# Second attention: scatter rounds one step earlier, and routing places and weights ahead of one clip

## The reference, cut to what matters

```python
x = x + _L1_xattn_ref(_layernorm(x), ctx_2048, mask, ...)    # 16 heads of 16, scores clipped to +-50
x = x + _L1_ffn_ref(_layernorm(x), gate_w, ...)
# in _L1_ffn_ref: E = 32 experts, K = 4 chosen for each token
logits = x @ gate_w.T + gate_b
topk_logits, topk_idx = jax.lax.top_k(logits, K)
topk_weight = jax.nn.softmax(topk_logits, axis=-1)
order = jnp.argsort(flat_idx)      # rows sorted by expert, then expert products, then summed with the weights
```

## Time and profile before

| what | value |
|---|---|
| median of 3 runs | 1764.74 us (1764.31 to 1765.02) |
| profiled execution, its own time | 1765.31 us |
| its span (first to last instruction) | 1763.6 us |
| second attention with routing, from the first apply to the start of the experts | about 1088 to 1431 us of the span |
| busy over the whole span | PE 86%, DVE 76%, ACT 61%, POOL 60% |

### The profile page before, as it was taken

The page is one execution under the profiler, slowest core; times in us unless marked ns, Lnnn a source line. Parts: engine busy times, 40 slices in busy tenths (PEclk is TensorE's granted clock), DMA queues, the critical chain, the costliest instruction groups (busy, mean ns, idle before and its releaser), DMA issues. The chain is left out here.

```text
span 1763.6 us, 43951 instructions
## 1 busy us (share of the span) xinstructions
PE 1519.7 (86%) x14968; PEld 1227.8 (70%) x14968; DVE 1345.9 (76%) x2949; ACT 1079.1 (61%) x3276; POOL 1053.9 (60%) x1063
## 2 busy tenths in 40 slices
PE   4999999999999999988988841899988249999966
PEld 4888888888888888865657730466656149999955
DVE  3898998999999999976644546489987328888876
ACT  3888888888888888863325620666552036666610
POOL 2667676767666666654764750027777736666642
PEclk9999999999999999998998975899997569999989
DMA  6600000000000000003235653002222855555557
GB/s 178 182 20 20 18 13 20 20 20 20 20 20 20 14 17 20 17 2 134 83 133 170 198 163 132 13 25 83 95 71 81 283 191 166 167 165 163 168 196 282
DMA packets 103082, 167.67 MB, mean 95 GB/s; under 512 B 20223, under 2 KB 75980, under 8 KB 102480
## 3 DMA queue, kind: packets, MB, share of 16 engines
q1 hardware_dynamic: 77136, 105.37, 19.3%
q0 software_dynamic: 22272, 56.15, 8.6%
q10 hardware_dynamic: 3456, 3.34, 0.6%
HBM read 95.31 MB, written 75.76 MB: 97 GB/s over the span
## 5 line engine op out<-in xcount | busy, mean ns | idle before, releaser
L438 POOL TENSOR_TENSOR w_down<-w_down,attn_rsum 128x1024 f32<-128x1024 f32 x256 | 483.9, 1895 | 234.9 <-DVE attn_rsum L397 233.9
L366 ACT ACTIVATE w_down<-attn_ps_s,attn_negmax 128x256 f32<-128x256 f32 x1024 | 469.6, 499 | 1.8 <-DVE attn_negmax L391 1.8
L402 DVE COPY w_down<-attn_ps_t 128x1024 f32<-128x1024 f32 x256 | 312.1, 1219 | 40.2 <-PE attn_ps_t L288 36.5
L391 DVE TENSOR_REDUCE attn_negmax<-attn_ps_s 128x4 f32<-128x1024 f32 x256 | 309.5, 1209 | 41.8 <-PE attn_ps_s L276 41.4
L961 POOL DMA_INDIRECT l_by_token<-layer_arena x240 | 240.1, 1000 | 150.1 <-issue 99.1
L276 PE MATMUL attn_ps_s<-ctx_d,attn_q_sb 64*128 64x256 f32 x2048 | 280.2, 386 | 2.1 <-ACT w_down L366 1.4
L302 PE MATMUL attn_ps_qo<-w_down,attn_vb 128*64 128x256 f32 x2048 | 250.6, 386 | 1.6 <-DVE w_down L402 1.3
L366 ACT ACTIVATION_READ_ACCUMULATOR w_down<-attn_ps_s,attn_negmax 128x1 f32 x1024 | 239.1, 233 | 0.0
L1130 POOL DMA_INDIRECT l_rows_in<-layer_arena,l_routing_group_slots x192 | 190.4, 991 | 57.6 <-issue 43.0
L288 PEld LDWEIGHTS attn_ps_t<-ident,w_down 64*128 64x128 f32 x4096 | 168.4, 138 | 77.6 <-issue 71.5
L276 PEld LDWEIGHTS attn_ps_s<-ctx_d,attn_q_sb 64*128 64x128 f32 x2048 | 209.6, 189 | 5.8 <-issue 2.8
(11 more groups left out here) (208 smaller groups left out, 2403.3 us busy)
## 6 DMA issues: line engine op xcount, KB each, us to landing
layer_arena<-l_rows_in SPq DMA_DIRECT2D x240, 136.0 KB, 2.3
w_gu<-l_by_token SPq DMA_DIRECT2D x32, 512.0 KB, 10.3
ctx_d<-in_ctx SPq DMA_DIRECT2D x64, 128.0 KB, 2.8
layer_arena<-l_by_token SPq DMA_DIRECT2D x32, 256.0 KB, 3.8
w_gu<-in_w_gu SPq DMA_DIRECT2D x16, 512.0 KB, 4.7
l_rows_in<-zeros SPq DMA_DIRECT2D x1, 4352.0 KB, 37.5
x_sb<-in_x SPq DMA_DIRECT2D x32, 128.0 KB, 2.5
w_down<-in_w_down SPq DMA_DIRECT2D x1, 4096.0 KB, 12.4
```

What stands on the lines that cost most here:

```text
L366: last = nc.scalar.activation(prob[:, n % 4, c, :], ps_s[:, n % 2, c, :], ACT.Exp, bias=negmax[:, n % 2, c:c + 1], accum_out=sums[:, n % 2 ...
L391: nc.vector.tensor_reduce(negmax[:, n % 2, :], ps_s[:, n % 2, :, :], AX.X, ALU.max, negate=True).then_inc(max_ready, 1)
L402: nc.vector.tensor_copy(prob_t[:, n // 2 % 2, n % 2, :, :, :].rearrange("p k c (d s) -> p d (k c) s", d=2), ps_t[:, :, :, :].rearrange("p ...
L438: nc.gpsimd.tensor_tensor(prob[:, n % 4, :, :], prob[:, n % 4, :, :], rsum[:, n % 2, :].unsqueeze(2).to_broadcast([P, 4, A_N]), ALU.mult). ...
```

## The change

`FIRST` falls from 10 to 9, and (5, 2) moves from the hand-written end of the list into its regular part, so that the order of the 32 rounds stays the same and each round stands one step earlier on POOL. In DVE's step with j = 1, `place_rows` and `weigh` move from behind the clip to ahead of it. The numbers in L1566 change with `in_order` (22 becomes 23).

```diff
-    FIRST = 2 * GT + 2
+    FIRST = 2 * GT + 1
     in_order = [(q, k) for q in range(NG) for k in range(m.K)][:NT - FIRST]
-    rounds = in_order + [(NG - 3, 2), (NG - 2, 0), (NG - 3, 3), (NG - 2, 1), (NG - 1, 0), (NG - 2, 2), (NG - 1, 1),
+    rounds = in_order + [(NG - 2, 0), (NG - 3, 3), (NG - 2, 1), (NG - 1, 0), (NG - 2, 2), (NG - 1, 1),
                          (NG - 2, 3), (NG - 1, 2), (NG - 1, 3)]
...
+            if j == 1 and gexists(it, g - 2):
+                rt.place_rows(dve, it, g - 2, gdone)
+                rt.weigh(dve, it, g - 2, gdone)
             if texists(it, r + 1):
                 clip(it, r + 1)
             if j == 2 and gexists(it, g + 2):
                 statistics(it, g + 2, stats_a, mv_a, vare_a, steps_a)
-            if j == 1 and gexists(it, g - 2):
-                rt.place_rows(dve, it, g - 2, gdone)
-                rt.weigh(dve, it, g - 2, gdone)
```

## The result

The changed kernel takes **1776.65 us** (median of 4 runs, 1776.02 to 1777.57) against 1764.53 us for the kernel before in the same measurement (4 runs, 1761.12 to 1765.02). The ratio is 1.0073, with a 95% interval from 1.0056 to 1.0091: slower, by 12.1 us. The forecast was 1777.5 us, with a range from 1768.5 to 1782. The profiled execution took 1776.62 us (span 1774.8), 11.3 more than that of before.

The account below looks back on a forecast made before the run. The prediction took DVE to set the steady pace, PE close behind, and group 7's chain to set the end. Terms 2.4 + 2.8 + 0.5 + 5.8 + 1.3 = +12.8 us gave 1777.5 us, range 1768.5 to 1782.

Parts of the forecast that it names:

- The two causes: The moved clip, through ACT and PE, in the steady part; POOL's queue at round (6, 0) at the end, +5.8 us.
- Steps 9 to 21, POOL's chain and the places: Steps 9, 13, 17, 21: POOL's chain starts `apply_a` at T0 + 17.96, T0 being the start of the places: +2.4 us.
- one coincidence: Step 25's slow L1104 beside POOL's L1907, taken to recur in steps 9 to 21, 0.56 us more on DVE each.
- ACT and PE: Moved clip delays exponentials and the query copy behind them on ACT; PE idles 2.8 us, at no further cost while clock holds.
- The clock, two falls in four: PE's new idle stretch halves its clock in two of steps 9, 13, 17, 21, 1.4 us each: +2.8 us.
- Steps 25 and 29: No `apply_a` follows them: 0 for step 25, +0.5 us for step 29, where L1104 lands beside POOL's L1907.
- The end: POOL waits at (6, 0) for group 6's weights, delaying tile 31's residual, group 7's chain and round (7, 0): +5.8 us.
- The waits: POOL idle some 7 us ahead of (6, 0), DVE over 5 ahead of tile 31's residual, POOL 5 at (7, 0).
- The ninth load: Nine, not eight, `w_gu` loads come with or after round (7, 0); 512 KB more delay the last round: +1.3 us.
- Faster: Rival: rounds end one step sooner and step 21's landing wait goes, 1758.5 us; chance 0.04.
- The clock held: Rival: no clock fall in steps 9 to 21, +10.0 us, 1774.7 us; chance 0.34, with or without the smaller terms.
- "L1104 at over 1 us": Sign expected in the new profile in steps 9 to 21: DVE's L1104 of `place_rows` slowed beside POOL's L1907.

Follow-up runs that it names:

- late_swap_2: Repeat on chip A of the changed kernel with late exponentials on ACT and rounds (5, 3) and (6, 0) exchanged: 1766.44 us, ratio 1.0009.
- late_exp: Changed kernel with ACT's exponentials behind the copy of the second half of the queries in steps 9, 13, 17, 21, 25; chip B: 1814.31 us, ratio 1.0012.
- after_3: The changed kernel, unaltered, measured again on chip A: 1775.14 us, ratio 1.0061.
- eight_loads: Changed kernel with eight, not nine, of the sixteen early expert-weight loads coming with or after round (7, 0); chip A: 1776.91 us, ratio 1.0072.
- late_clip: Kernel before with places and weights ahead of the clip and exponentials behind the query copy, no round moved; chip A: 1762.27 us, ratio 0.9984.
- swap_end: Changed kernel with rounds (5, 3) and (6, 0) exchanged, so (5, 3) stands in step 32; chip B: 1824.25 us, ratio 1.0087.
- late_swap: Changed kernel with exponentials behind the query copy and rounds (5, 3) and (6, 0) exchanged; chip C: 1818.18 us, ratio 0.9972.
- late_only: Kernel before with only the exponentials moved behind the copy of the second half of the queries in five steps; chip C: 1824.93 us, ratio 1.0012.
- after_2: The changed kernel, unaltered, measured on chip C: 1841.87 us, ratio 1.0113.
- clip_only: Kernel before with only places and weights moved ahead of the clip, no round moved; chip B: 1833.15 us, ratio 1.0125.
- before_2: The kernel before, unaltered, measured again on chip C: 1823.20 us, ratio 1.0005.
- first_only: Changed kernel with the clip back ahead of places and weights, rounds still one step earlier; chip B: 1825.95 us, ratio 1.0090.

## Why the prediction held, step by step

The two causes that the prediction named are the ones that the runs show, and its time lies 0.9 us from the measured one. That it lies so near is partly luck: terms that were too small and too large, and 1.55 us from outside the stage, make up for each other.

The account inside the stage, on chip A, from the table: up to clip 23 +5.84; from there to group 6's weights -1.87; from these to group 7's +6.32; to the experts +0.45. The sum is 10.74 us, and 1.55 us were lost ahead of the stage's second clip and 1.05 won back behind the start of the experts, which makes the 11.2 us of the span. The forecast sum was 12.8.

- *Steps 9 to 21, POOL's chain and the places, +2.4 forecast.* late_swap_2 has this cost without the ACT path: +3.37 at clip 23. The size was about right, the working in part not. In the changed kernel `apply_a` starts 18.30 to 18.62 us behind the start of the places (forecast 17.96), but waits for POOL in steps 9 and 17 only; in 13 and 21, where the clock fell, DVE is that late itself. In late_swap_2 it waits for POOL in all four, and starts 17.57 to 18.34 us behind: there POOL's chain sets the pace, as forecast. And L1104 ran 1.25 us in step 9 alone and 0.68 or 0.69 in the other five. In these five POOL's L1907 took the extra time, ahead of a round for which POOL had to wait 1.20 or 1.21 us for the weights anyway. That step failed: it took one coincidence for a rule and put 0.56 us on DVE in four steps, where it fell on DVE once. By the prediction's own working the term without it is about 0, so what makes up the 3.4 us is something else. In the first three steps 2.5 us of it stand at `apply_a`, where POOL takes 14.39 to 14.92 us from the round's start (forecast 14.30); 0.9 us lie between `apply_a` and the next step's places, where the prediction had no term. The size of this term was luck. (Of the seven rows of L1104 that it calls 0.68 us, the one of step 29 is 0.71.)
- *ACT and PE.* The forecast idle stretch of PE was 2.8 us, with the slow L1104 in it; without those 0.56 us 2.2, and the rows show 2.34 to 2.36, and 2.56 where L1104 was slow. Removing the path on ACT removes it: shown by late_exp. This path with its falls of the clock is the other 2.47 us at clip 23 (168.56 against late_swap_2's 166.09).
- *The clock, two falls in four, +2.8.* There were two, and a fall costs about 1.2 us on average (forecast 1.4). But the same kernel had three of those four steps fall in after_3: the count was a good guess, no more.
- *Steps 25 and 29, 0 and +0.5 forecast.* Measured -1.87. The kernel before had its own fall in step 25, at 1316; in the changed kernel the clock held there. In after_3 it fell at 1320, and this term is -0.38. On chip A the stretch from clip 23 to group 6's weights is 87.4 to 87.8 us in the three traces with a fall in step 25 (before, after_3, eight_loads) and 85.2 to 86.4 in the three without (changed, late_swap_2, late_clip). So what the changed kernel won here fits the fall that didn't come. Here the prediction was too high.
- *The end, +5.8.* From weights to weights +6.32, and round (7, 0) now follows group 7's weights by 0.33 us instead of 0.67: +5.98. The waits were forecast at 7, over 5, and 5 us, and are 7.95, 6.35 and 5.04. swap_end, late_swap and late_swap_2 take the residual's wait down to 1.02 or 1.03 us by an exchange of two rounds: shown.
- *The ninth load, +1.3.* Measured some 0.5 us, not clear of what single traces differ by. The term took the bandwidth price of 512 KB whole; in the trace the last round's wait for a landing grew from 3.95 to 4.37 us only. That the rest of the load lay beside POOL's own work is likely, but no run shows it.
- *The rivals.* Faster didn't come, for the reason given: group 7's weights, not the number of rounds, set (7, 0). Even in late_swap_2, with nothing in the way at (6, 0), it waits 3.39 us for them. The clock held in all four runs in which the exponentials are late and the clip is moved (late_exp, late_swap, late_swap_2, late_clip), where PE isn't idle at that place. Of the signs, "L1104 at over 1 us" came in one step of six.

The forecast for the stage was 2.1 us too high, and is made up of errors of both signs: 0.6 too low for steps 9 to 21 (5.2 for 5.84), 2.4 too high for steps 25 and 29, 0.2 too low from group 6's weights to round (7, 0), 0.5 too high behind (7, 0), where 0.79 us came and not 1.3. That the medians lie 12.1 us apart owes something to the 1.55 us from ahead of the stage, which no step of the prediction had. An execution with more falls, as after_3, gives +13.64 in the stage.

## What to carry to other kernels

Before an instruction is moved on one engine, follow what stands behind its consumer in the next engine's queue: the clip's own consumer, the exponentials, had time (late_only puts them later still, at no cost), but a copy queued behind them held the PSUM bank that PE needed next. A piece of work that needs a late result should not be put ahead of a short one that others wait for, if the queue is in order; exchanging two rounds at the end was worth 5 us of 6. With both mended the change of order gives nothing on chip A (ratio 1.0009) and at most 0.3% on chip C (0.9972), because the end hangs on group 7's own chain.

## What the runs showed of the hardware

**Who starts second pays.** DVE's L1104 (two SBUF inputs, 128 x 512) and POOL's L1907 start within 0.07 us of each other 50 times in the stage, over the 14 traces. In 12 of them POOL starts first, and DVE's instruction takes 1.23 to 1.25 us instead of 0.68; in 38 DVE starts first, and POOL's takes 1.20 to 1.26 instead of 0.72. There is no exception. Two pairs of the changed kernel:

```profile
1182.10 1.25 DVE L1104 TENSOR_TENSOR layer_arena<-layer_arena 128x512 f32<-128x512 f32 x1
...
1214.75 0.68 DVE L1104 TENSOR_TENSOR layer_arena<-layer_arena 128x512 f32<-128x512 f32 x1
```

```profile
1182.08 0.72 POOL L1907 TENSOR_TENSOR layer_arena<-x_sb,w_beta 128x256 f32<-128x256 f32 x1
...
1214.78 1.25 POOL L1907 TENSOR_TENSOR layer_arena<-x_sb,w_beta 128x256 f32<-128x256 f32 x1
```

A difference of 0.02 us decides which engine pays. In late_clip POOL starts 0.28 us behind DVE once, and takes 0.98 us: the less the two overlap, the less it costs. The Trainium skill (GPSIMD Engine Reference, section 8, Key points) says that the two contend for their SBUF interfaces when a VectorE instruction has two SBUF inputs; the traces agree, and in them the contention falls whole on the later one.

**PE's outputs come late behind an idle stretch, on two of three chips.** After PE's idle stretch in after_2 (chip C), on PE, ACT and DVE:

```profile
1219.82 1.10 PE L1580 MATMUL layer_banks<-w_v,w_gu 128*128 128x256 f32 x4 [2.57 <-ACT w_gu L1697]
...
1223.96 1.13 PE L1637 MATMUL layer_banks<-layer_arena,w_gu 128*64 128x34 f32 x32
1225.02 1.98 PE L1587 MATMUL layer_banks<-w_gu,w_k 128*128 128x512 f32 x4
...
1230.64 1.10 PE L1580 MATMUL layer_banks<-w_v,w_gu 128*128 128x256 f32 x4 [2.78 <-ACT w_gu L1713]
```

```profile
1229.81 0.69 ACT L1713 ACTIVATE w_gu<-layer_banks,w_bk 128x512 f32<-128x512 f32 x1 [2.71 <-DMA l_by_token<-layer_arena]
```

```profile
1228.35 0.26 DVE L1818 RECIPROCAL layer_arena<-layer_banks 128x16 f32<-128x16 f32 x1 [1.99 <-DMA layer_arena<-l_rows_in]
```

By its records PE has the outputs (L1637) done at 1225.1 and the second half of the keys (L1587) at 1227.0, at a granted clock of 1.00. Their readers start at 1228.35 and 1229.81, some 3 us later, and then PE waits for ACT in turn, 2.78 us more. The releasers in those rows are inferred, and no DMA feeds either instruction. This happens in clip_only, swap_end and after_2, 16, 16 and 22 us of DVE's idle time, at L1818 in or behind the steps in which PE had stood idle at L1580; not in the runs of the same two chips whose exponentials are late or whose clip is not moved, and not on chip A, where the idle stretches are as long. (Of a lesser kind are waits of 0.4 us and more at the clip L1811 with no releaser in the profile. They come in the three runs on B and C whose clip stands ahead of the places: before_2 7.4 us in five, first_only 3.7 in four, late_only 3.2 in three; beside them only late_swap has one, of 0.4. On chip A there are none.) So the idle stretch is needed for it (late_exp beside swap_end and clip_only), and a chip that does it. What holds the results back is open: the ends of matmuls are modelled in these records, so PE may have been slower than they say. On chip A the changed kernel loses 10 to 12 us, on chip C 18. Up to group 6's weights it is 4.0 and 16.2 us, and these late outputs are what stands out in the trace on C beside those on A; that they are the whole difference is not shown.

**Chips differ.** The unchanged kernel took 1765, 1811 and 1824 us on the three chips. In the kernel before the second clip stands at 1120.48 on A and 1147.91 on C, behind code that no experiment touched. So only times from one chip are compared in this document where a cause hangs on them.
